# A causal mask moved from TensorE to a select on GpSimd, and a DMA queue put in another order

## What is computed

```python
x = x + 0.5 * ffn(layernorm(x))      # 8 experts of 128x128, the best 2 of each token, mixed by their weights
x = x + attn(layernorm(x))
x = x + 0.5 * ffn(layernorm(x))

# attn: 8 heads of width 128, 2 groups of keys and values, latent width 32
q = (x @ wq).reshape(B, T, 2, 4, 128)
k_lat, v_lat = x @ wk_down, x @ wv_down            # 2 x 32 columns each
k, v = k_lat @ wk_up, v_lat @ wv_up
scores = einsum('bqhrd,bkhd->bhrqk', q, k) * scale
scores = where(causal, scores, finfo.min)          # a query sees no later key
y = einsum('bhrqk,bkhd->bqhrd', softmax(scores), v)
```

## Time and profile before

| | |
|---|---|
| median of 3 runs | 727.15 us (719.2, 727.15, 729.8) |
| the profiled execution | 725.95 us |
| its span, first to last instruction | 724.1 us |
| mean granted clock of TensorE | 0.869 |
| slot 0 of batch 0 (first score) starts at | 96.4 us |
| batches 1, 2, 3 start at | 242.2, 398.1, 561.7 us |
| last score at | 687.95 us |

### The profile page before, as it was taken

The page is one execution under the profiler, slowest core; times in us unless marked ns, Lnnn a source line. Parts: engine busy times, 40 slices in busy tenths (PEclk is TensorE's granted clock), DMA queues, the critical chain, the costliest instruction groups (busy, mean ns, idle before and its releaser), DMA issues. The chain is left out here.

```text
span 724.1 us, 10881 instructions
## 1 busy us (share of the span) xinstructions
PE 559.3 (77%) x3526; PEld 277.5 (38%) x3526; DVE 426.6 (59%) x1538; ACT 357.5 (49%) x843; POOL 154.5 (21%) x257
## 2 busy tenths in 40 slices
PE   2726578998987689888994779989894888897935
PEld 2625243344432334344342343434432433343323
DVE  5462765786655475775563456866753577565225
ACT  3233262466665445756463534657653546467612
POOL 2131200143001002510013201531012220043313
PEclk9957667699999689998697697999998899999957
DMA  4002010000110000011000000001100000000000
GB/s 122 0 14 56 15 40 17 1 17 16 45 45 6 18 1 1 16 34 48 24 1 23 16 15 1 1 5 42 44 1 23 16 16 1 1 17 14 16 0 16
DMA packets 23818, 14.59 MB, mean 20 GB/s; under 512 B 5640, under 2 KB 23632, under 8 KB 23760
## 3 DMA queue, kind: packets, MB, share of 16 engines
q1 hardware_dynamic: 23184, 13.49, 6.9%
q10 hardware_dynamic: 576, 0.39, 0.2%
HBM read 3.78 MB, written 2.10 MB: 8 GB/s over the span
## 5 line engine op out<-in xcount | busy, mean ns | idle before, releaser
L706 ACT ACTIVATE prob<-bank,exp_scale 128x512 f32<-128x512 f32 (+3 forms) x384 | 214.9, 583 | 248.7 <-PE bank L1186 183.7
L926 DVE CUSTOM_DVE_ANT_0 masked<-bank,mask_qk 128x128 f32<-128x128 f32 (+3 forms) x256 | 122.7, 486 | 110.6 <-PE bank L1170 109.6
L1170 PE MATMUL bank<-k_stack,q_stack 96*128 96x512 f16 (+3 forms) x384 | 138.6, 366 | 41.5 <-DVE m_part L929 11.9
L1183 PE MATMUL bank<-q_stack,k_stack 98*128 98x512 f16 (+3 forms) x384 | 136.0, 361 | 35.9 <-DMA q_stack<-mT_lo 30.4
L929 DVE TENSOR_REDUCE m_part<-bank 128x1 f32<-128x512 f32 x128 | 87.5, 684 | 72.1 <-PE bank L1170 71.7
L575 POOL TENSOR_TENSOR pair_sum<-dve_sum,scaled 128x256 f32<-128x256 f32 x64 | 46.9, 733 | 282.9 <-DVE dve_sum L899 265.0
L1202 PE MATMUL bank<-prob,v_lat 128*32 128x512 f32 (+3 forms) x768 | 90.6, 546 | 0.5 <-ACT prob L706 0.5
L1205 PE MATMUL bank<-prob,ones 128*32 128x512 f32 (+3 forms) x768 | 87.0, 528 | 0.0
L1183 PEld LDWEIGHTS bank<-q_stack,k_stack 98*128 98x128 f16 x384 | 38.5, 101 | 120.8 <-issue 48.5
L664 ACT ACTIVATE scaled<-bank,gate 128x128 f32<-128x128 f32 x256 | 72.7, 373 | 20.7 <-PE bank L1097 6.6
L1095 PE MATMUL bank<-we_hi,xT_hi 128*128 128x512 f32 x128 | 67.9, 531 | 16.6 <-ACT scaled L664 12.1
(11 more groups left out here) (132 smaller groups left out, 705.6 us busy)
## 6 DMA issues: line engine op xcount, KB each, us to landing
q_stack<-q_hi SPq DMA_DIRECT2D x120, 32.0 KB, 1.8
x<-in_L_attn_x SPq DMA_DIRECT2D x8, 256.0 KB, 2.9
out_x<-x SPq DMA_DIRECT2D x8, 256.0 KB, 2.4
q_stack<-q_lo SPq DMA_DIRECT2D x60, 32.0 KB, 1.9
k_stack<-k_hi SPq DMA_DIRECT2D x32, 32.0 KB, 1.8
prob<-in_L_ffn_expert_weights SPq DMA_DIRECT2D x1, 512.0 KB, 4.3
x<-in_L_attn_wq SPq DMA_DIRECT2D x1, 512.0 KB, 6.0
x<-in_L_attn_wo SPq DMA_DIRECT2D x1, 512.0 KB, 7.0
```

The lines of the kernel that those rows point to most:

```text
L706: nc.scalar.activation(into, bank[ST + n % NST][:, 0:w], ACT.Exp, scale=exp_scale[:, 0:1]).then_inc(p_ready, 1)
L926: V.tensor_tensor_reduce(out=masked[:, m % 2, 0:w], in0=seen, in1=mask_qk[:, CH - w:CH], op0=ALU.add, op1=ALU.max, scale=1.0, scalar=LOWES ...
L1170: mm(into[:, 0:w], q_stack[0:MROW, c, g * NR + r, (i % TC) * P:(i % TC + 1) * P], k_stack[0:MROW, b % 2, g, k:k + w], start=True, stop=Tru ...
L1183: last = mm(into[:, 0:CH - off], k_stack[:, b % 2, g, j * P:(j + 1) * P], q_stack[:, c, g * NR + r, off:CH], start=True, stop=not on_diago ...
```

## The change

The mask matmul goes away, with its two tiles and four of the nine steps that write constants. In its place POOL runs one select over the four heads' 128x128 squares in `prob`, after the exponential, which writes zero where the key is later than the query (`keep_causal`; 128 partitions x 4 x 128 elements, 64 times). The weighing of values of a diagonal group now waits for this select (`p_kept`) and not for the exponential. `PV_LAG` goes from 3 to 4, and joins and the last back unit follow by one slot. `stack_slot` holds a quad's queries back until the slots in which the same quad of the batch before is done: quad 3's go from slots 69 to 72 into slots 2, 5, 8 and 11 of the next batch, quad 2's from 63 to 66 into 66, 69, 72 and 75. Batch 0 stays as it was.

```diff
-PV_LAG = 3
+PV_LAG = 4
-CONST_STEPS = 9
+CONST_STEPS = 5
...
-    return b * NS + (47, 103)[c]
+    return b * NS + (48, 104)[c]
...
+def stack_slot(n, g, r, planned):
+
+    b, c = divmod(n, NC)
+    q = c * NKV + g
+    free = (b - 1) * NS + QSTART[q] + NR * QTILES[q] + 2 + 3 * r
+    return max(planned, free) if b else planned
...
             for _r in range(NR):
-                PLAN["stack_queries", _k + 1 + _r].append((_n, _g, _r))
+                PLAN["stack_queries", stack_slot(_n, _g, _r, _k + 1 + _r)].append((_n, _g, _r))
...
-            step(nc.gpsimd.memset(ident_b[:], 0.0))
-            select(ident_b[:], 0, [[-1, P]], 1)
...
-            step(nc.gpsimd.memset(mask_kq[:], 0.0))
-            select(mask_kq[:], 0, [[1, P]], -1, ALU.is_ge, MASKED)
...
+            def keep_causal(b, q, j):
+
+                pool.wait_ge(p_ready, group_end(b, q, j) + 1)
+                square = prob[:, GROUP[b, q, j] % NPG, :, 0:P]
+                nc.gpsimd.affine_select(out=square, in_=square, compare_op=ALU.is_ge, fill=0.0, base=0,
+                                        pattern=[[0, NR], [1, P]], channel_multiplier=-1).then_inc(p_kept, 1)
...
             for s in range(LO, HI):
+                if s - 1 + PV_LAG in PV_AT and on_diagonal(*PV_AT[s - 1 + PV_LAG][1:]):
+                    keep_causal(*PV_AT[s - 1 + PV_LAG])
                 if s - 2 in END_AT:
                     normalise(END_AT[s - 2])
...
-                last = mm(into[:, 0:CH - off], k_stack[:, b % 2, g, j * P:(j + 1) * P],
-                          q_stack[:, c, g * NR + r, off:CH], start=True, stop=not on_diagonal(q, j))
-                if on_diagonal(q, j):
-                    last = mm(into[:, 0:P], ident_b[:], mask_kq[:], start=False, stop=True)
-                last.then_inc(st_done, 1)
+                mm(into[:, 0:CH - off], k_stack[:, b % 2, g, j * P:(j + 1) * P],
+                   q_stack[:, c, g * NR + r, off:CH], start=True, stop=True).then_inc(st_done, 1)
...
-                pe.wait_ge(p_ready, group_end(b, q, j) + 1)
+                if on_diagonal(q, j):
+                    pe.wait_ge(p_kept, DIAGONAL[b, q, j] + 1)
+                else:
+                    pe.wait_ge(p_ready, group_end(b, q, j) + 1)
```

More of the change, by code:

```diff
@@ L76 @@
 TILE = {k: i for i, k in enumerate(TILES)}
-LO, HI = -72, NALL + 48
+LO, HI = -72, NALL + 49
 def join_slot(n):
     b, c = divmod(n, NC)
-    return b * NS + (47, 103)[c]
+    return b * NS + (48, 104)[c]
 def tile_slot(f, n, t):
@@ L168 @@
 GROUP = {g: i for i, g in enumerate(GROUPS)}
+DIAGONAL = {g: i for i, g in enumerate(g for g in GROUPS if on_diagonal(*g[1:]))}
 def first_query(q, j):
@@ L413, in macaron @@
         p_ready = sem("p_ready")
+        p_kept = sem("p_kept")
         pv_done = sem("pv_done")
```

4 lines of the change are left out of this document (1 added, 3 removed).

## The result

The changed kernel takes 702.6 us in the median (702.1 to 703.2, four runs) beside 726.9 for the kernel before (719.2 to 729.8, four runs): a ratio of 0.968, 95% interval [0.961, 0.976]. That is faster by 24 us, where the prediction said 41.6; the time lies just above its range. The profiled execution took 703.23 us, with a span of 701.5 us and a mean granted clock of 0.865 (before 0.869).

The account below looks back on a forecast made before the run. PE was taken to set the pace with short waits, plus a few long holes from SP's queue. -27.7 - 5 - 12 + 4 + 0.4 = -40.3 us led to 685.5 us, forecast 678 to 692, outer range 670 to 702.

Parts of the forecast that it names:

- step 3: Removing 256 mask matmuls on PE, priced at 0.06 us each: -12 us, between 6 and 18 gained.
- Step 1: SP's queue: rows of maxima go ahead of quad 3's queries, closing three 9.9 us holes at batch ends: -27.7 us.
- step 2: PE's clock: 14 us at the lower level behind the holes return to full clock: -5 us, between 0 and 7.
- Step 4: The 64 selects on POOL, 0.9 us each, mostly covered by the weighing's later place: +4 us, between 0 and 10.
- Step 5: Kernel end: select and handovers before the last weighing, +1.1 us, less most of 1 us back: net +0.4.
- A: Rival: holes close only in part, PE meeting the experts' banks and DVE sooner; half given back: 702 us, chance 0.10.
- B: Rival: mask matmuls were hidden, their removal worth 2 instead of 12: 696 us, chance 0.17 with small shortfalls.
- C: Rival: clock and mask terms pay in full, select never late: 676 us, down to 670, chance 0.15.
- D: Rival: the select on POOL is the bound, each of 64 weighings waiting for it: 742 us, chance 0.03.
- E: Rival: DVE is held while POOL selects, 34 us of delay: 719 us, chance 0.07 together with A in full.

Follow-up runs that it names:

- e1: Kernel before with only the new order of SP's queue (`stack_slot`), mask matmuls and lag 3 kept, no select: 690.3 us, ratio 0.945.
- e9: Same kernel as e1, the new queue order alone, measured again on another chip: 694.1 us, ratio 0.952.
- e18: Changed kernel with the joins back in slots 47 and 103, a repeat of e14 on another chip: 685.5 us, ratio 0.946.
- e17: Kernel before with new queue and lag 4, joins left in 47 and 103, mask matmuls, no select, a repeat of e12: 685.4 us, ratio 0.945.
- e12: Kernel before with new queue and lag 4, joins left in 47 and 103, mask matmuls, no select: 690.1 us, ratio 0.946.
- e14: Changed kernel with the joins back in slots 47 and 103: 684.2 us, ratio 0.948.
- e7: Kernel before with new queue, lag 3 and old joins, but neither mask matmul nor select, so later keys count: 693.6 us, ratio 0.955.
- e13: Changed kernel, nothing altered, measured again on another chip: 699.1 us, ratio 0.964.
- e2: Kernel before with new queue, lag 4 and joins from slot 48, mask matmuls, no select: 692.3 us, ratio 0.952.
- e16: Same kernel as e2, measured again on another chip: 695.5 us, ratio 0.961.
- e6: Changed kernel without its select, so neither mask matmul nor select and later keys count: 697.2 us, ratio 0.959.
- e15: Changed kernel with the mask matmuls put back beside the select, a second measurement: 694.6 us, ratio 0.961.
- e8: Kernel e2 with each mask matmul issued twice, no select: 702.4 us, ratio 0.968.

## Why the prediction was wrong, point by point

The prediction failed at two steps. It had no term for the joins, which the change moves by one slot: that costs 12 to 15 us beside the select. And its step 3 gave 12 us to the removal of the mask matmuls with the clock held constant: the exchange of mask for select is worth nothing.

**What bounds the kernel.** Right: PE sets the pace, and the holes were the queue's, not an engine's.

**Step 1, the queue, -27.7, and step 2, the clock, -5.** Right in the mechanism, and a little small: together 32.7 where e1 and e9 measured 40 and 35 by their ratios, 37 by their medians. The row's DMAs, the first score and the granted clock are as forecast. The cover for the twelve DMAs of queries held: the one wait for `q_hi`, 2.3 us, is in slot 5 of batch 0, whose queries were not moved. Step 2 counted 14 us at half clock behind the holes. The executions of the kernel before have 197 to 202 us at half clock in the mean of each chip, those of e1 and e9 155 and 161, so some 40 less. At 0.34 us each that is up to 14 us, less what lay inside the holes, where PE had nothing to do.

**Step 3, the mask matmuls, -12.** The second failure. The price of 0.06 us from one pair of starts was too high, since over whole quads at full clock it is 0.028 to 0.037, and 7.2 to 9.5 for all. More important, step 2 knew the clock only behind the holes and step 3 had it constant. The 22 to 33 us more at half clock in e18 than in e17 cost as much again, so the exchange is worth about nothing: 0.1 us between their medians, 0.7 between the mean ratios of e12 and e17 (0.9456) and of e14 and e18 (0.9466). Without any select it is the same: e7 without mask matmuls and e9 with them have 0.955 and 0.952.

**Step 4, the select, +4.** The duration was put at 0.9 us and is 0.635, between the bounds. By the Trainium skill, page "GPSIMD Engine Reference", section 4.1, one-input operations run roughly at line rate, which the prediction turned into an estimate of 0.5. The measured 0.635 lies between that and the 0.9: with the 294 ns of rows 7 for 128 columns it is 0.114 us for each further square and 0.18 for the fixed part, where the prediction had 0.19 and 0.105. The 1.2 GHz of the page's section 1 would be 0.107 for a square, as an estimate, so the rule holds for the slope; what it leaves out is the fixed part. The lag does hide it: 0.2 us of PE's time, once. With lag 3 it would have been 5.4 us. No cost of the select shows in any pair: the term is 0 within some 4 us.

**Step 5, the end, +0.4.** From the exponential to the weighing are 0.76 us where 0.05 were the earlier trace rows, so the select with its handovers is +0.7 and not +1.1. What the last score gains by standing ahead of a weighing was not measured by itself.

**The step that is missing.** The main failure is an edit that got no price. The diff moves the joins by one slot, and the prediction speaks of the lag's effect on the weighing but gives neither joins nor lag a term. The joins cost 12 to 15 us in the pair e13, e14, and 8 us beside the mask matmuls (e2 and e16 against e12 and e17 by their ratios, 0.957 and 0.946). What they cost shows as PE's stops for banks that DVE frees later, and as half clock behind them. The lag gives 2 us back by the ratios and 4 in the pair e9, e12. Sum by the mean ratios of each kernel's two measurements, times 727 us: -38 for the queue and its clock, -2 for the lag, +1 for the exchange, +14 for the joins: -25, where 24 was measured. It closes because each term is the difference of two neighbouring kernels; a single term is good to some 4 us.

**The rivals.** A, B, C, D and E said 702, 696, 676, 742 and 719. The time is that of A, but that is luck, since its mechanism isn't there: the holes closed in full. PE's waits for DVE and ACT, which A has growing, add up to 112 us in the kernel before, to 115 in e9 with the queue alone and to 129 in the changed kernel: they grew by the rest of the change, not by the closing of the holes. B is nearest to the truth for the mask, though for another reason: the matmuls weren't hidden, their gain was lost at the lower clock. E's price is wrong, but the hold that it names is real, and the prediction read the wrong rows for it. DVE's sums are as in rows 10 beside the 64 selects:

```profile
L914 DVE SCALAR_TENSOR_TENSOR dve_sum<-bank,gate,scaled x128: 329/341/351, 29.6 to 696.2; 128x128 f32<-128x128 f32 x128
```

But these take one tile from a bank. The small steps of the norm statistics take theirs from SBUF, and they do get held. In the kernel before, beside the product of a quad's output:

```profile
464.76 1.27 POOL L589 TENSOR_TENSOR yT<-o_sb,r_t 128x512 f32<-128x512 f32 x1 [1.07 <-issue]
...
465.18 0.86 DVE L811 TENSOR_TENSOR diff<-stats 128x4 f32<-128x4 f32 x1
```

In the changed kernel, beside a select:

```profile
314.75 0.63 POOL L593 TENSOR_SCALAR_AFFINE_SELECT prob<-prob 128x512 f32<-128x512 f32 x1 [2.90 <-ACT prob L721]
...
315.00 0.41 DVE L826 TENSOR_TENSOR diff<-stats 128x8 f32<-128x8 f32 x1
```

The step, a difference of two tiles in SBUF, takes 0.17 us elsewhere in both kernels, and here it ends within 0.03 us of the operation on POOL both times. The Trainium skill, page "SBUF — State Buffer", section "Who interferes with whom", has DVE and GpSimd under an exclusive lock on a shared pair of ports, which an instruction of DVE with at most one input in SBUF does not need outside some faster modes. The traces agree, with the sums on the one side and this step on the other. It costs little here: DVE instructions that took at least 0.06 us more than the median of their form are 16 in the kernel before, 4.5 us in all, and 17 in the changed one, 3.9 us, of which 0.6 us beside selects. That is all there is of E's 34 us, and DVE's busy time rose from 426.6 us to 427.2.

The range ended 0.6 us too low, since it had no case for a loss from an edit outside the four that were priced.

## What to carry to other kernels

An edit that "only follows", one slot for a later stage here, wants its own look: which buffer does it hold longer, who takes that buffer next, and what stands behind it on the engine that frees it. A shared pool that hands out what comes free first changes the owners of all later uses too, and a stop of 1 to 2 us on TensorE can cost more than itself, where the granted clock falls behind it. And a change that takes small matmuls away is to be judged with its granted clock beside it, over whole stretches and not from two starts.

The best version is the changed kernel with the joins in slots 47 and 103, at 0.948 [0.941, 0.954] and 0.946 [0.940, 0.951]; the kernel before with the new queue and lag 4 alone, with nothing on GpSimd, is as fast: 0.946 [0.940, 0.952] and 0.945 [0.940, 0.951].

## What was not expected of the hardware

After an idle time of 1.1 to 1.7 us on PE in slots 52 and 53 the granted clock was 0.50 to 0.61 over the next 4.3 to 5.2 us, three times of three; where the same matmuls had no such stop it was 1.00. It is no rule for stops of that length: behind 2.35 us of idle time before 468.70 the same kernel kept 1.00.

The kernels without mask matmuls spend more time at half clock than those with them. By the mean of all executions e6 has 174 us and e16 153, e7 183 and e9 161, e13 181 and e15 146, e18 162 and e17 140: four of four comparable pairs. Twice the mask matmuls did not lower it further: e8 has 149 us, e2 and e16 145 and 153. That the mask matmuls keep the clock up by filling PE's time is the natural reading, but it wasn't tried with other filling work and so stays argued. A us at half clock cost 0.34 to 0.43 us in this kernel. It would be 0.5 if the rate of the matmuls set the pace everywhere; that ACT and DVE, which go on at their own pace, set it elsewhere is argued, not shown.

Small operations of DVE on tiles in SBUF did not end before an operation of POOL that ran beside them: a step of 0.17 us took 0.41 beside a select and 0.86 beside a product, while DVE's work on banks beside them kept its time.
